# Routing scratch moved into the logits' PSUM banks, both clears of the expert rows issued at the start, and a new list of places

## The reference, cut to what matters

```python
xn = layernorm(x)
s = attention(xn)                       # diagonal masked
g = silu(moe2(xn))                      # 8 experts of width 256, top 2 by a softmax gate, all computed
x = x + s * g
xn = layernorm(x)
s = mamba(xn) + xn                      # conv, x_proj, dt, selective scan: 256 channels x 16 states x 512 steps
g = silu(moe1(xn))                      # 8 experts of width 512; each token goes to argmax(xn @ centroids.T)
x = x + s * g
# moe1: out = alpha * y_expert + (1 - alpha) * xn, alpha = sigmoid(xn . centroid[expert])
```

## Time and profile before

| | us |
|---|---|
| median of 3 runs | 970.54 |
| lowest and highest | 968.39, 974.35 |
| the profiled execution, device time | 969.87 |
| its span, first to last instruction | 968.1 |
| its mean granted clock of PE | 0.893 |
| DVE busy | 808.3 (83%) |
| PE busy | 782.5 (81%) |
| POOL busy | 598.3 (62%) |
| ACT busy | 591.6 (61%) |

### The profile page before, as it was taken

One profiled execution on the slowest core, in us unless ns is written; L12 is line 12 of the kernel. 1 busy time (PEld: TensorE's weight loads), 2 busy tenths in 40 slices (PEclk: granted clock), 3 DMA queues, 4 the chain that ended last, 5 costly groups with the idle time before them and its releaser, 6 DMA issues.

```text
span 968.1 us, 15221 instructions
## 1 busy us (share of the span) xinstructions
PE 782.5 (81%) x4404; PEld 551.6 (57%) x4404; DVE 808.3 (83%) x1499; ACT 591.6 (61%) x1230; POOL 598.3 (62%) x564
## 2 busy tenths in 40 slices
PE   4999977868999899867899699867999767459972
PEld 2667645545676567545567477545677454237641
DVE  3253776999999999998999889988999889999772
ACT  2535654747586867657577857567577846366641
POOL 0000215759385948488577958478576968797673
PEclk9997987987999999978999899978999897659995
DMA  7800183212232332041233332042233432324641
GB/s 243 276 1 1 43 266 94 55 61 62 56 98 81 105 88 77 23 125 49 77 99 89 104 92 78 22 116 57 75 91 84 122 96 70 90 72 132 181 116 46
DMA packets 87155, 89.89 MB, mean 93 GB/s; under 512 B 9138, under 2 KB 60194, under 8 KB 86562
## 3 DMA queue, kind: packets, MB, share of 16 engines
q1 hardware_dynamic: 85026, 84.73, 31.0%
q0 software_dynamic: 2048, 4.20, 1.4%
HBM read 66.99 MB, written 21.91 MB: 92 GB/s over the span
## 4 chain that ended last, share of the span: by engine, by line
DVE 34%; PE 26%; issue 18%; POOL 14%; ACT 5%; SPq 2%; DMA 1%; DVEq 0%; POOLq 0%; ACTq 0%
DVE st L1454 10%; PE work L907 5%; POOL st L1636 5%; PE work L913 5%; DVE b_row L1443 3%; DVE acc L1312 3%; POOL y L1643 3%; DVE cv L1341 3%; DVE dbu L1443 2%; POOL xs_dram L1601 2%; POOL fe L1619 2%; PE work L821 2%; PE work L948 1%; PE work L1010 1%; PE work L938 1%
## 5 line engine op out<-in xcount | busy, mean ns | idle before, releaser
L1636 POOL TENSOR_TENSOR st<-st,Cs 128x512 f32<-128x512 f32 x249 | 317.1, 1282 | 163.8 <-DVE st L1454 139.1
L1051 ACT ACTIVATE dA<-delta,Aneg 128x512 f32<-128x512 f32 x256 | 176.6, 723 | 38.4 <-DVE st L1454 36.5
L1454 DVE TENSOR_TENSOR_SCAN st<-dA,dbu 128x512 f32<-128x512 f32 x128 | 154.9, 1210 | 10.2 <-ACT dA L1051 9.8
L907 PE MATMUL work<-xnT,w_w1a 128*128 128x512 f32 x256 | 139.5, 652 | 14.7 <-ACT hid L1051 12.4
L1454 DVE TENSOR_TENSOR_SCAN st<-dA,b_row 128x512 f32<-128x512 f32 x123 | 148.8, 1210 | 2.4 <-DVE acc L1312 1.5
L913 PEld LDWEIGHTS work<-w_w2a,hid 128*128 128x128 f32 x1024 | 132.5, 205 | 28.5 <-issue 10.5
L913 PE MATMUL work<-w_w2a,hid 128*128 128x128 f32 x1024 | 135.6, 290 | 8.7 <-DVEq L1368 7.9
L1643 POOL TENSOR_TENSOR y<-y,st 128x512 f32<-128x512 f32 x105 | 134.9, 1285 | 4.3
L1051 ACT ACTIVATE hid<-work,w_b1a 128x512 f32<-128x512 f32 x128 | 87.5, 689 | 75.4 <-PE work L907 70.9
L978 PE MATMUL yacc<-w_ident,st 128*128 128x128 f32 x448 | 78.2, 306 | 29.2 <-POOL st L1636 29.2
L1312 DVE SCALAR_TENSOR_TENSOR acc<-work,gates,acc 128x128 f32<-128x128 f32 x256 | 70.9, 340 | 34.6 <-PE work L913 34.4
(11 more groups left out here) (212 smaller groups left out, 1308.3 us busy)
## 6 DMA issues: line engine op xcount, KB each, us to landing
Cs<-c_dram SPq DMA_DIRECT2D x128, 256.0 KB, 3.4
hs<-w1f_dram SPq DMA_DIRECT2D x60, 258.0 KB, 3.0
xs_dram<-fe SPq DMA_DIRECT2D x34, 256.0 KB, 4.1
xs_in<-xs_dram SPq DMA_DIRECT2D x60, 64.0 KB
ys_dram<-ys SPq DMA_DIRECT2D x12, 256.0 KB, 3.7
w_w1f<-in_w1f_dram SPq DMA_DIRECT2D x1, 2064.0 KB, 7.8
w1f_dram<-w_w1f SPq DMA_DIRECT2D x1, 2064.0 KB, 7.3
x_in<-in_x_dram SPq DMA_DIRECT2D x8, 256.0 KB, 4.0
```

The source lines that it names most:

```text
L907: last = mm(w[:], W["w1a"][:, i * 128:(i + 1) * 128], xnT[:], start=True, stop=True)
L1051: return nc.scalar.activation(out, in_, func, **k)
L1454: V.tensor_tensor_scan(state(s), dA[:, s % DECAYS], (dbu0, rows_bank(n, b))[h][:], 0.0, ALU.mult, ALU.add).then_inc(sig["scan"], 1)
L1636: G.tensor_tensor(state(s), state(s), Cs[:, b.of(NS, n) % C_BUFS], ALU.mult).then_inc(sig["P"], 1)
```

## The change

The scratch of `gl` and `gate` moves into slices of the bank that holds the logits (`beside(w, k)`); the bank is now freed at the end of `gate`, no longer in `gl`. `first_max` in `sc` keeps `eq` in the scores' bank, and a second reduce puts the maximum there too. `al` loses its addition: ACT adds the 1 with a second small instruction. `rk` and `tile_table` keep their scratch in rk's bank, freed at their end; `ntile` is computed twice (once to SBUF, once to PSUM); the last addition writes `gpos` directly and a cast goes. SP issues `clear_rows(1)` right after `clear_rows(0)`. All places, lags and banks of ROWS, OWN and OWN_BANKS are new.

```diff
-    ("P", "dve", 4, -0.21092, -4, -2, 6, None),
-    ("A", "gl", 0, 0.09322, 2, 0, 7, 0),
-    ("A", "gate", 0, 0.10736, 2, 0, 7, None),
-    ("H", "rk", 0, 0.63740, 3, 0, 2, 3),
-    ("P", "save", 0, 0.01296, 1, 0, 0, None),
...
+    ("P", "dve", 4, -0.26971, -4, 1, 6, None),
+    ("A", "gl", 0, 0.06886, 1, -1, 7, 3),
+    ("A", "gate", 0, 0.09958, 2, -1, 7, None),
+    ("H", "rk", 0, 0.59884, 3, 1, 2, 3),
+    ("P", "save", 0, -0.59534, 1, 0, 0, None),
...
             sp.wait_ge(prep_dve, 1)
             clear_rows(0)
+            clear_rows(1)
...
-                    go(gp[:], gt[:], ACT.Exp).then_inc(sig["g_exp"], 1)
+                    go(w[:, 5 * n:6 * n], w[:, n:2 * n], ACT.Exp).then_inc(sig["g_exp"], 1)
...
-                    go(alpha[:, b.n % 4], am[:], ACT.Exp, scale=-1.0).then_inc(sig["a_exp"], 1)
+                    p = alpha[:, b.n % 4]
+                    go(p, am[:], ACT.Exp, scale=-1.0).then_inc(sig["a_first"], 1)
+                    act.wait_ge(sig["a_first"], b.of(1, 1))
+                    go(p, p, ACT.Identity, bias=1.0).then_inc(sig["a_exp"], 1)
...
+            def beside(w, k):
+                return w[:, k * NT * E:(k + 1) * NT * E].rearrange("p (i e) -> p i e", e=E)
...
-                    dve.wait_ge(sig["g_in"], b.of(1, 1))
-                    dve.sem_inc(fr, 1)
...
+                    gt, eq, oh2, gp = (beside(w, k) for k in (1, 2, 3, 5))
+                    total = w[:, 6 * NT * E:6 * NT * E + NT]
...
+                    V.tensor_tensor(gates[:], gp, spread8(gr[:]), ALU.mult).then_inc(sig["gates"], 1)
+                    dve.wait_ge(sig["gates"], b.of(1, 1))
+                    dve.sem_inc(free_of(g, ("gl", 0), b), 1)
...
-                    first_max(g, wl, am, eq, ohr[:, par])
+                    top = w[:, 2 * NT * E:2 * NT * E + NT]
+                    V.tensor_reduce(top, beside(w, 0), AX.X, ALU.max)
+                    first_max(g, beside(w, 0), am[:], beside(w, 1), ohr[:, par])
...
-                    lk(g, V.tensor_scalar(p, p, 1.0, None, ALU.add))
...
-                    r = posr[:, 0:NT]
+                    r = beside(w, 2)
...
+                more = room(96, 128, E, ROOM).rearrange("p (e k) -> p e k", e=E)
+                count_t, endt, ahead = (room(160 + k * E, 128, E) for k in range(3))
+                texf, past, at = (room(192 + k * ST, 1, ST) for k in range(3))
...
+                V.tensor_reduce(ntile[:], more, AX.X, ALU.add)
+                lk(g, V.tensor_reduce(count_t, more, AX.X, ALU.add))
...
-                V.tensor_copy(gpos[:, par], moved[:]).then_inc(sig["pos"], 1)
+                lk(g, V.tensor_tensor(gpos[:, par].rearrange("p b i -> p (b i)"), moved,
+                                      posf[:].rearrange("p b i -> p (b i)"), ALU.add))
+                dve.sem_inc(sig["pos"], 1)
```

More of the change, by code:

```diff
@@ L570, in build @@
         ohb = sb("ohb", [128, 2, NT, E], BF16)
-        more = sb("more", [128, E, ROOM])
         ntile = sb("ntile", [128, E])
-        endt = sb("endt", [128, E])
         ones8 = sb("ones8", [128, E])
-        posr = sb("posr", [128, 2 * NT, E])
         posf = sb("posf", [128, 2, NT])
         pos = sb("pos", [128, 2, NT], U32)
-        moved = sb("moved", [128, 2, NT])
-        shift8 = sb("shift8", [128, E])
         gpos = sb("gpos", [128, 2, 2, NT], U32)
-        upto = sb("upto", [1, ST, E])
-        texf = sb("texf", [1, ST])
         skip = sb("skip", [1, ST])
@@ L763, in do @@
                                  ).then_inc(sig["w1f_out"], 16)
-                    clear_rows(1)
             def clear_rows(p):
@@ L1073, in a_step @@
                     act.wait_ge(sig["g_in"], b.of(1, 1))
-                    go(gp[:], gt[:], ACT.Exp).then_inc(sig["g_exp"], 1)
+                    w = bank(g, step, b)
+                    n = NT * E
+                    go(w[:, 5 * n:6 * n], w[:, n:2 * n], ACT.Exp).then_inc(sig["g_exp"], 1)
                 elif name == "q":
@@ L1254, in first_max @@
             def first_max(g, p, m, e, hot):
-                lk(g, V.tensor_reduce(m[:], p[:], AX.X, ALU.max))
-                lk(g, V.tensor_tensor(e[:], p[:], spread8(m[:]), ALU.is_equal))
-                lk(g, V.tensor_tensor(e[:], e[:], tiles8(W["first"]), ALU.mult))
-                lk(g, V.tensor_reduce(gr[:], e[:], AX.X, ALU.max))
-                lk(g, V.tensor_tensor(hot[:], e[:], spread8(gr[:]), ALU.is_equal))
+                lk(g, V.tensor_reduce(m, p, AX.X, ALU.max))
+                lk(g, V.tensor_tensor(e, p, spread8(m), ALU.is_equal))
+                lk(g, V.tensor_tensor(e, e, tiles8(W["first"]), ALU.mult))
+                lk(g, V.tensor_reduce(gr[:], e, AX.X, ALU.max))
+                lk(g, V.tensor_tensor(hot, e, spread8(gr[:]), ALU.is_equal))
+            def beside(w, k):
+                return w[:, k * NT * E:(k + 1) * NT * E].rearrange("p (i e) -> p i e", e=E)
             def tiles8(t):
@@ L1281, in a_step @@
                     filled(dve, g, step, b)
-                    wl = w[:, 0:NT * E].rearrange("p (i e) -> p i e", e=E)
-                    lk(g, V.tensor_reduce(gm[:], wl, AX.X, ALU.max))
-                    V.tensor_tensor(gt[:], wl, spread8(gm[:]), ALU.subtract).then_inc(sig["g_in"], 1)
-                    dve.wait_ge(sig["g_in"], b.of(1, 1))
-                    dve.sem_inc(fr, 1)
-                elif name == "gate":
-                    dve.wait_ge(sig["g_exp"], b.of(1, 1))
-                    emptied(dve, g, ("gl", 0), b)
-                    lk(g, V.scalar_tensor_tensor(eq[:], gt[:], 0.0, tiles8(W["first"]), ALU.is_equal, ALU.mult))
-                    lk(g, V.tensor_reduce(gr[:], eq[:], AX.X, ALU.max))
-                    lk(g, V.tensor_tensor(oh1[:], eq[:], spread8(gr[:]), ALU.is_equal))
-                    lk(g, V.scalar_tensor_tensor(gt[:], oh1[:], -3.0e38, gt[:], ALU.mult, ALU.add))
-                    first_max(g, gt, gm, eq, oh2)
-                    lk(g, V.tensor_tensor(oh1[:], oh1[:], oh2[:], ALU.add))
-                    lk(g, V.tensor_tensor(gp[:], gp[:], oh1[:], ALU.mult))
-                    lk(g, V.tensor_reduce(gm[:], gp[:], AX.X, ALU.add))
-                    lk(g, V.tensor_scalar(gm[:], gm[:], 1e-12, 2.0, ALU.max, ALU.mult))
@@ new lines, in a_step @@
+                    gt = beside(w, 1)
+                    lk(g, V.tensor_reduce(gm[:], beside(w, 0), AX.X, ALU.max))
+                    V.tensor_tensor(gt, beside(w, 0), spread8(gm[:]), ALU.subtract).then_inc(sig["g_in"], 1)
+                elif name == "gate":
+                    w = bank(g, ("gl", 0), b)
+                    gt, eq, oh2, gp = (beside(w, k) for k in (1, 2, 3, 5))
+                    total = w[:, 6 * NT * E:6 * NT * E + NT]
+                    dve.wait_ge(sig["g_exp"], b.of(1, 1))
+                    dve.wait_ge(sig["g_in"], b.of(1, 1))
+                    lk(g, V.scalar_tensor_tensor(eq, gt, 0.0, tiles8(W["first"]), ALU.is_equal, ALU.mult))
+                    lk(g, V.tensor_reduce(gr[:], eq, AX.X, ALU.max))
+                    lk(g, V.tensor_tensor(oh1[:], eq, spread8(gr[:]), ALU.is_equal))
+                    lk(g, V.scalar_tensor_tensor(gt, oh1[:], -3.0e38, gt, ALU.mult, ALU.add))
+                    first_max(g, gt, gm[:], eq, oh2)
+                    lk(g, V.tensor_tensor(oh1[:], oh1[:], oh2, ALU.add))
+                    lk(g, V.tensor_tensor(gp, gp, oh1[:], ALU.mult))
+                    lk(g, V.tensor_reduce(total, gp, AX.X, ALU.add))
+                    lk(g, V.tensor_scalar(gm[:], total, 1e-12, 2.0, ALU.max, ALU.mult))
@@ L1377, in a_step @@
                     filled(dve, g, step, b)
-                    before, count = w[:, 0:NT * E].rearrange("p (i e) -> p i e", e=E), w[:, NT * E:(NT + 1) * E]
-                    r = posr[:, 0:NT]
+                    before, count = beside(w, 0), w[:, NT * E:(NT + 1) * E]
+                    r = beside(w, 2)
                     lk(g, V.tensor_tensor(r, before, tiles8(W["room"]), ALU.add))
-                    if par:
-                        lk(g, V.tensor_tensor(more[:], count.unsqueeze(2).broadcast_to([128, E, ROOM]),
-                                              W["full"][:].unsqueeze(1).broadcast_to([128, E, ROOM]), ALU.is_gt))
-                    dve.sem_inc(free_of(g, step, b), 1)
                     lk(g, V.tensor_tensor(r, r, ohr[:, par], ALU.mult))
                     lk(g, V.tensor_reduce(posf[:, par], r, AX.X, ALU.add))
-                    V.tensor_copy(pos[:, par], posf[:, par]).then_inc(sig["put_at"], 1)
+                    last = V.tensor_copy(pos[:, par], posf[:, par])
+                    last.then_inc(sig["put_at"], 1)
                     if par:
-                        tile_table(g, b.n // 2 % 2)
+                        tile_table(g, b.n // 2 % 2, count, w)
+                    else:
+                        dve.wait_ge(sig["put_at"], b.of(1, 1))
+                    dve.sem_inc(free_of(g, step, b), 1)
                 elif name == "du":
@@ new lines, in tile_table, with room @@
```

(31 more changed lines are left out.)

37 lines of the change are left out of this document (7 added, 30 removed), and 586 rows, old and new, of tables (OWN, OWN_BANKS, ROWS, sig).

## The result

| | before | changed |
|---|---|---|
| median, us | 972.44 (4 runs) | 928.11 (4 runs) |
| lowest and highest | 968.39, 974.75 | 925.63, 930.57 |
| ratio with its 95% interval | | 0.9548 (0.9497 to 0.9599) |
| span of the profiled execution | 968.1 | 928.7 |
| its mean granted clock of PE | 0.893 | 0.918 |

What follows compares the result with a forecast made beforehand. The prediction took DVE's instruction stream to bound the middle, with a stall at the scan's start. From a span of 968.1 us it took 25 for DVE's waits and 9.5 for the stall, forecasting 936, range 919 to 953.

Steps and rivals of the forecast that it cites:

- What bounds the kernel: From 165 to about 866 us, DVE's instruction stream plus some 5 us idle per 100 sets the time.
- Part 1, waits behind POOL: Small DVE operations with SBUF inputs wait for POOL; moving operands to PSUM takes 31.4 us off DVE, 25 off the run.
- How much of a saving on DVE reaches the end: Share of DVE's saved time that shortens the run: taken as 0.8, with 0.5 if PE or POOL take over.
- Small operations in PSUM: Extra time of some 200 moved DVE operations that write PSUM: taken as 0, 5 us kept for the range.
- ACT's added instruction: One more ACT instruction per batch, 1.6 us in all, beside ACT's idle time: 0 for the end.
- Part 2, the stall: At the scan's start POOL waits 13.14 us for C's second row behind 18 clears; issuing them early gains 9.5 us.
- Part 3, banks and places: Longer-held gl and rk banks cost 0 given the new list's room; the rest of the list 0, bounds -8 and +8.
- The rival on held banks: PE waits for gl's or rk's bank until DVE finishes; at 6 us per period the run takes 984; chance 0.04.
- The sum: 968.1 - 25 - 9.5 = 933.6 us of span, 935.4 with the time around it, stated as 936.
- PE takes over: Rival: PE becomes the limit in the middle, half of the DVE saving is lost, 948 us; chance 0.16.

Runs made afterwards that it cites:

- eq_sbuf: The changed kernel with one scratch tile, eq, back in SBUF and banks held as in the change: 935.33 us against 929.85 for the changed kernel beside it.
- held_late: The kernel before, scratch in SBUF and old places, with only the banks of the gate's logits and the ranking freed later: 991.55 us, ratio 1.0199.
- psum_alone: The kernel before with only the scratch moved to PSUM and alpha's +1 on ACT, old places and clears: 968.36 us, ratio 0.9959.
- held_new: New places and early clears, scratch in SBUF, the two banks freed as late as in the change: 939.76 us, ratio 0.9632.
- changed_again: The changed kernel, unaltered, measured once more beside later runs: 929.85 us, ratio 0.9555.

## Why the prediction was right, and where it was not

- **What bounds the kernel**: right. DVE's stream sets the middle; 32 us less on it came with 22.4 us less in periods 1 to 6, 3.7 a period where about 4 were named.
- **Part 1, waits behind POOL**: the mechanism is shown by `eq_sbuf`, and the amount off DVE was right, 32.4 us for 31.4, but partly by luck: at the old places the scratch alone took 19.8 us off (788.5), because the wait went on to the cast to `ohb`; at the new ones the list had taken 15 us of the waits away before, and 4.1 us went on to the cast to `pos`. With scratch and later release together the step at the new places is worth 19.3 us (947.4 to 928.1), where I took 25. How much of a saving on DVE reaches the end, I had put at 0.8. With the banks held alike it is 23.2 us of 24.5 at the old places (`held_late` to `psum_alone`), 9.9 of 14.9 at the new ones (`held_new` to `changed_again`) and 5.5 of 10.3 in `eq_sbuf`: 0.5 to 0.95.
- **Small operations in PSUM**: 199 ns for 192 in place. Some 7 ns on about 200 operations are 1.4 us; I took 0 and held 5 open. Start to start, chained operations follow in 0.22 to 0.24 us in both places (first `gate` of both traces), so nothing more hides between them. The Trainium skill's Perfetto Trace Analysis, section "Optimizing Scalar/DVE Operations", with some 65 ns more for DVE on PSUM, is not borne out here: the measured durations decide.
- **ACT's added instruction**: ACT has 590.1 us busy for 591.6; no cost.
- **Part 2, the stall**: first product at 133.93 inside my 128.7 to 135, third at 136.37 inside 130 to 137.6, DVE's gain in the stretch 123 to 165 is 9.3 us. The term of 9.5 is about right for the changed kernel's first period (10.2), too high at the old places (6.0), and too low as what the edit is worth at the new ones (15.2), where `save` stands ahead of C's first row.
- **Part 3, banks and places**: the step that was off. A cost of 0 for the held banks was right for the changed kernel: PE waits 1.8 us for them. It was right with less room than I reckoned with: the ranking's bank has 5 or 6 PE steps and 6.3 us, not 7 or 8 steps. But I priced the list at 0 with bounds of 8 either way, and it is worth 18 us with the clears alone (965.7 to 947.4) and 36 on top of clears and scratch. The rival on held banks had its mechanism right and its condition right (the distance in the list): at the old places it eats 19.3 us. That the list is the part which removes this cost stood in my own text and did not reach the sum.
- **The sum** of 936 came near 928 by luck in part, because errors offset each other: scratch and clears as separate gains came to 34.5 us, while without the list they bring 7.7; the list was missing. Along one path the terms measure 6.0 for the clears, 18.3 for the list and 19.3 for the scratch, where I had 9.5, 0 and 25. The new places by themselves, with neither clears nor scratch, were not run.
- **PE takes over**: not seen in the time. PE has 93.20 us of 100 from 250 to 350 and 91.80 from 450 to 550, and still the scratch brought 10 to 19 us.

## What to carry to other kernels

Look at the mean of the same small VectorE operation by form: where one form has 0.19 us and another 0.6 to 0.9, count its inputs in SBUF and look at what GpSimd runs at that moment. One operand in PSUM removes the wait, but the wait can jump to the next operation with two inputs in SBUF or to a cast from SBUF to SBUF, so move the whole chain. The small reduces did not wait here and need no move. Scratch in a matmul bank prolongs its holding; price that by moving the release alone, and give the bank's next user a later place before judging the scratch.

## What was not expected of the hardware

- A cast from SBUF to SBUF of 128x32 or 128x4 elements waits for GpSimd like the two-input operations: 1107 ns for 182 (`ohb`), 685 for 163 with its source in PSUM (`pos`). My sum had moved only the forms that showed a wait in the trace of before. The Trainium skill, SBUF — State Buffer, section "Who interferes with whom", counts casts and operations with a scalar among those that can take the port pair shared with GpSimd, beside its rule on two SBUF inputs; the runs agree, and so does the addition to `alpha` (0.50 to 1.10 us where it starts during an operation of POOL, 0.16 elsewhere).
- A few microseconds of PE waiting in the start (7.8) came with a granted clock of 0.83 for 0.92 in the stretch from 62 to 123, and the first scan step was 13 us later, not 8. In `psum_alone` the same waits and the same first scan step (140.3) go with a clock of 0.86, so how much of the difference is the clock's is open.
- A small reduce from SBUF to SBUF never waited for GpSimd: 0.186 to 0.188 us in 7 executions that started during an operation of POOL.
